# Values of two steps on end, the shifts' parts on GpSimd, and a reordered second QKV stage in a two-layer transformer kernel

## The reference, cut to what matters

```python
q = apply_rope(q, 0)
k = apply_rope(k, 0)
scores = jnp.einsum('bhqd,bhkd->bhqk', q, k) / math.sqrt(HEAD_DIM)
scores = jnp.where(causal[None, None, :, :], scores, jnp.float32(-1e+20))
attn = jax.nn.softmax(scores, axis=-1)
out = jnp.einsum('bhqk,bhkd->bhqd', attn, v)
...
scores = jnp.einsum('bhfc,bhtc->bhft', k, q)
attn = jax.nn.softmax(scores, axis=-2)
vals = jnp.einsum('bhft,bhfc->bhtc', attn, v)
```

## Time and profile before

| | us |
|---|---|
| median of three executions | 1273.25 |
| lowest, highest | 1272.96, 1280.2 |
| profiled execution | 1285.09 |
| its span (first to last instruction) | 1283.3 |

### The profile page before, as it was taken

The page is one execution under the profiler, slowest core; times in us unless marked ns, Lnnn a source line. Parts: engine busy times, 40 slices in busy tenths (PEclk is TensorE's granted clock), DMA queues, the critical chain, the costliest instruction groups (busy, mean ns, idle before and its releaser), DMA issues.

```text
span 1283.3 us, 21563 instructions
## 1 busy us (share of the span) xinstructions
PE 1192.6 (93%) x6800; PEld 744.0 (58%) x6800; DVE 915.8 (71%) x2958; ACT 661.6 (52%) x1015; POOL 396.2 (31%) x521
## 2 busy tenths in 40 slices
PE   4999999999889998999989999999998999989988
PEld 1775443444358997545878644443332889855478
DVE  5778897999527868663777798998880578676365
ACT  1732574666545644444545136666666356445542
POOL 1433431221144520115624434122123445002261
PEclk9897696999899999899999958998897999989999
DMA  9555221131001014100241742112200100430001
GB/s 301 189 147 125 84 76 26 27 78 50 2 1 52 2 34 99 60 2 1 83 166 40 194 122 76 27 27 60 68 3 1 34 19 1 99 92 2 1 10 58
DMA packets 40053, 81.44 MB, mean 63 GB/s; under 512 B 6044, under 2 KB 7580, under 8 KB 39532
## 3 DMA queue, kind: packets, MB, share of 16 engines
q1 hardware_dynamic: 39944, 80.06, 21.8%
HBM read 50.02 MB, written 28.13 MB: 61 GB/s over the span
## 4 chain that ended last, share of the span: by engine, by line
PE 71%; DVE 14%; issue 5%; DMA 4%; ACT 3%; POOL 2%; SPq 1%; DVEq 0%; ACTq 0%; POOLq 0%
PE bank L1060 17%; PE bank L927 12%; PE bank L833 6%; PE bank L835 6%; PE bank L834 6%; PE bank L1041 5%; DVE maxes L1280 5%; PE bank L819 3%; DVE unused L1276 3%; PE bank L1035 3%; PE bank L937 2%; DVE features L1209 2%; PE bank L858 2%; PE bank L909 1%; PE bank L860 1%
## 5 line engine op out<-in xcount | busy, mean ns | idle before, releaser
L1528 ACT ACTIVATE probs<-bank 128x1024 f32<-128x1024 f32 (+3 forms) x416 | 366.0, 911 | 278.3 <-PE bank L1041 195.4
L927 PE MATMUL bank<-ops 48*128 48x512 f32 (+3 forms) x960 | 315.3, 432 | 10.5 <-DVE maxes L1280 3.4
L1276 DVE CUSTOM_DVE_ANT_0 unused<-bank,causal 128x128 bf16<-128x128 f32 (+3 forms) x640 | 279.1, 486 | 44.7 <-PE bank L927 40.7
L1660 POOL TENSOR_SCALAR_AFFINE_SELECT probs<-probs 128x256 f32<-128x256 f32 (+1 forms) x256 | 119.4, 467 | 575.5 <-ACT probs L1528 574.5
L927 PEld LDWEIGHTS bank<-ops 48*128 48x128 f32 (+1 forms) x960 | 160.6, 205 | 194.3 <-DVE maxes L1276 77.3
L1060 PE MATMUL bank<-probs,v_mem 128*17 128x512 f32 (+6 forms) x1920 | 256.2, 542 | 1.4 <-ACT heads_raw L1515 0.8
L1280 DVE TENSOR_REDUCE maxes<-bank 128x1 f32<-128x512 f32 x320 | 207.2, 684 | 50.3 <-PE bank L927 49.3
L1041 PE MATMUL bank<-ops 50*128 50x512 f32 (+2 forms) x640 | 181.7, 464 | 8.0 <-DMA ops<-shiftT 4.6
L1041 PEld LDWEIGHTS bank<-ops 50*128 50x128 f32 x640 | 89.9, 205 | 68.0 <-issue 35.4
L833 PE MATMUL bank<-ops,xT 128*128 128x512 f32 (+1 forms) x288 | 114.0, 396 | 6.7 <-DVE xT L1119 2.6
L1119 DVE TENSOR_TENSOR xT<-bank,xT 128x512 fp32r<-128x512 f32 (+1 forms) x96 | 61.5, 644 | 75.5 <-ACT xT L1390 75.4
(11 more groups left out here) (128 smaller groups left out, 1903.8 us busy)
## 6 DMA issues: line engine op xcount, KB each, us to landing
query_rows_dram<-ops SPq DMA_DIRECT2D x48, 256.0 KB, 4.3
ops<-query_rows_dram SPq DMA_DIRECT2D x64, 192.0 KB, 4.4
w_odd<-staging_wqkv SPq DMA_DIRECT2D x4, 1536.0 KB, 6.8
x<-x_dram SPq DMA_DIRECT2D x16, 256.0 KB, 4.1
ops<-features SPq DMA_DIRECT2D x64, 64.0 KB, 2.0
ops<-ops SPq DMA_DIRECT2D x16, 256.0 KB, 3.0
out_dram<-x SPq DMA_DIRECT2D x16, 256.0 KB, 2.0
staging_wqkv<-wqkv_dram SPq DMA_DIRECT2D x2, 1536.0 KB, 14.2
```

Of the source, the lines that this page charges most:

```text
L927: last = mm(dst[:, h * w:(h + 1) * w], queries(a, u)[rows, t // 4, hi, t % 4 * P:(t % 4 + 1) * P], keys(a, u, hi)[rows, HALF * kp:HALF * k ...
L1276: V.tensor_tensor_reduce(unused[:, masked % 3, 0:w], part, causal[:, HALF - w:], 1.0, NEG, ALU.add, ALU.max, dst).then_inc(s["max_done"].s ...
L1528: A.activation(probs[:, e % 6, :, 0:cols], scores[:, 2 * (e % 2):2 * (e % 2) + 2, 0:cols], ACT.Exp, scale=a.scale).then_inc(s["exp"].sem, 1)
L1660: G.affine_select(out=p, in_=p, compare_op=ALU.is_ge, fill=0.0, base=0, pattern=pattern, channel_multiplier=-1).then_inc(s["masked"].sem, 1)
```

## The change

It does six things.

1. In the rotated attention the values of two steps stand on end too: at every odd step those of the steps three and two before it. The standard attention keeps its order.
2. `probs` has 8 places instead of 6.
3. The high and low part of a shift are made by POOL in the rotated attention (a copy and a subtraction, in POOL's list at the step in which the last maximum of that half is read). In both attentions the parts are those of the maximum itself, and the rows beside the keys hold minus one.
4. The two halves of a maximum are joined by a reduction over one operand (a view of both halves) in place of the maximum of two operands.
5. In the rotated attention the turning of a shift follows its last maximum by 6 banks instead of 3; `slack` goes from 4 to 1, so that as many items stand ahead of the first step as before.
6. The second QKV stage makes block (3, 0) ahead of the values, splits the first value products, and starts the ring later by another table; the second `load_shifts` of unit 0 goes ahead of the rows of block (2, 0).

```diff
-SHIFT_DELAY = 3
...
+        self.shift_delay = 6 if self.rope else 3
...
-            order = [(0, 0), (1, 0), first, (3, 0), (0, 1), (1, 1), (3, 1), second, (2, 1), (2, 0)]
-            self.ring_in = {4: (0, 0, 1, 1), 5: (1, 1, 1, 1), 7: (0, 0, 1, 1), 8: (1, 2, 2, 2), 9: (1, 2, 2, 1)}
+            order = [(0, 0), (1, 0), (3, 0), first[:2], (0, 1), (1, 1), (3, 1), first[2:], second, (2, 1), (2, 0)]
+            self.ring_in = {6: (1, 1, 1, 1), 7: (1, 1), 8: (1, 1, 1, 1), 9: (1, 2, 2, 2), 10: (1, 2, 2, 0)}
...
-A0 = Attention("rot", 32, 8, 16, 0.25, 2, True, ahead=1.07, slack=4)
+A0 = Attention("rot", 32, 8, 16, 0.25, 2, True, ahead=1.07, slack=1)
...
+PROBS = 8
...
                 load_shifts(b, QKV1, 0, 0)
-                for j, g in ((2, 1), (2, 0)):
-                    rows_of_block(b, j, g)
+                rows_of_block(b, 2, 1)
                 load_shifts(b, QKV1, 0, 1)
+                rows_of_block(b, 2, 0)
...
-                    if a.row_tiles == 2:
-                        if a.lag <= g < a.units * ns + a.lag:
-                            value(g - a.lag)
-                    elif g % 2 == 0 and g > a.lag and g - a.lag < a.units * ns:
+                    if (g - a.lag) % 2 == 1 and g > a.lag and g - a.lag < a.units * ns:
                         value(g - a.lag - 1)
                         value(g - a.lag)
...
-                    if n + 1 in a.max_banks_of:
+                    if n + 1 in a.max_banks_of and not (a.rope and n + 1 == a.max_banks_of[0]):
                         shift_parts(b, st, u, a.max_banks_of.index(n + 1))
...
                 if c == 1:
-                    V.tensor_tensor(mx, mx, maxes[:, u % 2, 1, 0:nh, 4:8], ALU.max).then_inc(s["shift_step"].sem, 1)
+                    both = maxes[:, u % 2, :, 0:nh, 4:8].rearrange("p k h t -> p h t k")
+                    mx = maxes[:, u % 2, 1, 0:nh, 0:4]
+                    V.tensor_reduce(mx.unsqueeze(3), both, AX.X, ALU.max).then_inc(s["shift_step"].sem, 1)
+                if a.rope:
+                    return
...
-                            if e >= 6:
+                            if e >= PROBS:
...
+            def shift_parts(b, u, c):
...
+                G.tensor_copy(hi, mx).then_inc(step.sem, 1)
+                pool.wait_ge(step.sem, step.at(b, 3 * u + 1 + 2 * c))
+                G.tensor_tensor(lo, mx, hi.bitcast(F32), ALU.subtract).then_inc(s["shift"].sem, 1)
...
+                    for (u, c), at in a.shift_parts_at.items():
+                        if a.rope and at == g:
+                            shift_parts(b, u, c)
```

More of the change, by code:

```diff
@@ L195, in plan_ring @@
         per = len(self.max_banks)
-        start = self.max_banks_of[0] + SHIFT_DELAY + self.slack
+        start = self.max_banks_of[0] + self.shift_delay + self.slack
         catch_up = sum(s[3] for s in self.steps[:3]) / sum(s[3] for s in self.steps)
@@ L217, in push @@
                 if n + 1 in self.max_banks_of:
-                    due_m.append([(u, self.max_banks_of.index(n + 1)), SHIFT_DELAY])
+                    due_m.append([(u, self.max_banks_of.index(n + 1)), self.shift_delay])
                 done += 1
@@ L238, in plan_ring @@
         self.ring_len = len(self.ring)
+        where = {item: s for s, step in enumerate(self.ring_at) for slot in step for item in slot}
+        self.shift_parts_at = {(u, c): where.get(("max", u, n - 1), -1)
+                               for u in range(self.units) for c, n in enumerate(self.max_banks_of)}
         self.norm_at = [i for i, item in enumerate(self.ring) if item[0] == "norm"]
-A0 = Attention("rot", 32, 8, 16, 0.25, 2, True, ahead=1.07, slack=4)
+A0 = Attention("rot", 32, 8, 16, 0.25, 2, True, ahead=1.07, slack=1)
 A1 = Attention("std", 8, 8, 32, 1.0, 1, False, ahead=1.07, slack=12)
@@ L337, in build @@
         v_mem = sb("v_mem", [P, NT * 8 * 33])
-        probs = sb("probs", [P, 6, 2, HALF])
+        probs = sb("probs", [P, PROBS, 2, HALF])
         w_odd = sb("w_odd", [P, 2, KC * 768], F32R)
@@ L772, in _ @@
                 load_ones(QKV1)
-                for j, g in ((0, 0), (1, 0), (3, 0), (0, 1), (1, 1), (3, 1)):
+                for _, j, g in [p for p in A1.products if p[0] == "qk" and p[1] != 2]:
                     rows_of_block(b, j, g)
                 load_shifts(b, QKV1, 0, 0)
-                for j, g in ((2, 1), (2, 0)):
-                    rows_of_block(b, j, g)
+                rows_of_block(b, 2, 1)
                 load_shifts(b, QKV1, 0, 1)
+                rows_of_block(b, 2, 0)
                 after(b, QKV1)
@@ L1060, in value @@
                         last = mm(heads[a.head_rows * h:a.head_rows * h + a.dim + 1, q0 - HALF * c:HALF],
-                                  v[:, j, a.kv_head(u, r, i), :], probs[:, e % 6, n, first:first + w],
+                                  v[:, j, a.kv_head(u, r, i), :], probs[:, e % PROBS, n, first:first + w],
                                   start=(j == 0), stop=(j == 4 * c + 3))
@@ L1524, in attention @@
                             act.wait_ge(s["scored"].sem, s["scored"].at(b, e + 1))
-                            if e >= 6:
-                                act.wait_ge(s["pv"].sem, s["pv"].at(b, a.step_of(e - 6) + 1))
-                            A.activation(probs[:, e % 6, :, 0:cols], scores[:, 2 * (e % 2):2 * (e % 2) + 2, 0:cols],
+                            if e >= PROBS:
+                                act.wait_ge(s["pv"].sem, s["pv"].at(b, a.step_of(e - PROBS) + 1))
+                            A.activation(probs[:, e % PROBS, :, 0:cols], scores[:, 2 * (e % 2):2 * (e % 2) + 2, 0:cols],
                                          ACT.Exp, scale=a.scale).then_inc(s["exp"].sem, 1)
@@ L1636, in chain @@
                             turn_late(b, 4)
+            def shift_parts(b, u, c):
+                a, s = A0, qs[QKV0]
+                nh, m, step = a.unit_heads, a.unit_heads * 4, s["shift_step"]
+                mx = maxes[:, u % 2, 1, 0:nh, 0:4] if c else maxes[:, u % 2, 0, 0:nh, 0:4]
+                if c == 0:
+                    pool.wait_ge(s["max_done"].sem, s["max_done"].at(b, u * a.unit_max_ops + a.max_ops_to[a.max_banks_of[c] - 1]))
+                else:
+                    pool.wait_ge(step.sem, step.at(b, 3 * u + 2))
+                if 2 * u + c >= 2:
+                    pool.wait_ge(s["shiftT"].sem, s["shiftT"].at(b, 2 * u + c - 1))
+                hi = shifts[:, c, 0:m].rearrange("p (h t) -> p h t", h=nh)
+                lo = shifts[:, c, m:2 * m].rearrange("p (h t) -> p h t", h=nh)
+                G.tensor_copy(hi, mx).then_inc(step.sem, 1)
+                pool.wait_ge(step.sem, step.at(b, 3 * u + 1 + 2 * c))
+                G.tensor_tensor(lo, mx, hi.bitcast(F32), ALU.subtract).then_inc(s["shift"].sem, 1)
             def attention(b, st):
@@ L1640, in attention @@
                 ns = len(a.steps)
-                for g in range(a.units * ns):
+                for g in range(-1, a.units * ns):
+                    for (u, c), at in a.shift_parts_at.items():
+                        if a.rope and at == g:
+                            shift_parts(b, u, c)
+                    if g < 0:
+                        continue
                     u, k_ = divmod(g, ns)
@@ L1693 @@
         "x": a["L0_attn_x"],
-        "tables": np.concatenate([np.tile(cos.T, (16, 1)), np.tile(sin.T, (16, 1))], axis=1), "ones": np.ones((2, 8 * SEQ), np.float32),
+        "tables": np.concatenate([np.tile(cos.T, (16, 1)), np.tile(sin.T, (16, 1))], axis=1), "ones": -np.ones((2, 8 * SEQ), np.float32),
         "ffn_w": a["L0_ffn_W"].T, "ffn_a": a["L0_ffn_lora_A"], "ffn_b": a["L0_ffn_lora_B"].T,
```

9 lines of the change are left out of this document (5 added, 4 removed).

## The result

The changed kernel took 1385.76 us (median of four executions, 1381.23 to 1389.45), against 1273.11 us for the kernel before: ratio 1.0881, 95% interval 1.0811 to 1.0951, 113 us more. The forecast was 1298 us, in a range from 1268 to 1324. The sign was right; the size was less than a quarter of what happened.

What follows compares the result with a forecast made beforehand. DVE and PE were taken to hold each other up through the ring of three banks. Terms 19.7 + 0.3 + 3.8 + 3.0 - 2.0 = +24.8 us on the median 1273.25 gave 1298 us, range 1268 to 1324.

Steps and rivals of the forecast that it cites:

- the clock: Rotated attention: about 12% of each 186 us stretch at half clock, unchanged there; 11.6 full-clock units x 1.7 = +19.7 us.
- The clock falls more often: Rival: PE waits more in each unit, so three more half-clock stretches on top of the sum; 1321 us, chance 0.14.
- The pairs' gaps: Rotated attention's ring: six pairs of values leave DVE idle 4.8 us a unit, for 1.96 now; unit 29.9 us.
- this case: The prediction's own case: +24.8 us on the median, 1298 us; reaching from 1283 to 1308, chance 0.60.
- PE is the limit after all: Rival: pairs shorten PE's work by at most 2.1 us a unit; 1254 us, chance 0.11.
- Gain and loss cancel: Rival: DVE's waits grow only by the 1.17 us of work it loses, unit 28.3; 1278 us, chance 0.15.
- The shifts' parts: Rotated attention: DVE loses 1.34 us a unit and gains a 0.17 us reduction, leaving 25.13 us of work.
- POOL is late nowhere but at the end of the ring: POOL's added instructions cost nothing, except at the ring's end: +0.3 us for both sequences.
- The start: Start of the rotated attention: the shift's copy moves later, so the first score is 1.9 us later; +3.8 us for two sequences.
- The end: End of the rotated attention: a cycle of two steps takes 4.7 us in place of 4.2; +3.0 us (0 to 5).
- The second QKV stage: Its end: shift rows' DMAs moved ahead, one ring bank less for the last product; -2.0 us for both sequences (0 to -7.2).

## Why the prediction was wrong

**The step that failed is the clock.** The prediction took 12% of each stretch at half clock from the kernel before, "11.6 units" at full clock, and let the change alter nothing there. The changed kernel has no unit at full clock. A middle unit grew by 7.7 us (29.5 to 37.2). Of these, 1.43 are the pairs' gaps at full clock, by the two runs with five added matmuls, less 0.17 for the shorter DVE work. The rest, some 6.4 us, comes with 18.5 us more of half clock. Single values bring all of it back; wide added matmuls bring the clock back and most of the time.

**The rival was named, and priced too low.** "The clock falls more often" had 0.14 and 1321 us, from three more stretches like the one of the earlier trace rows. What it describes is what happened, and its count was wrong: not three more in two attentions but two or three falls in every middle unit. The prediction held it against this rival that most units do without falls. But the pairs make the same stretches without values in every unit alike. What counts in these stretches was not separated: PE stands there for a part of the time (0.9 of 3.86 us), and what it makes is narrow. With pairs, five or 13 wide matmuls a unit end nearly all falls and 48 narrow ones do not, which speaks for what PE makes. In the kernel before, 16 narrow ones end them, which speaks for the standing.

The Trainium skill, TensorE: Matmul & The Clock Gate, section on psum-queue depth-cycling, puts clock changes down to short PE stops between groups of matmuls. The stretch at 239.30 agrees (0.9 us of standing). The two ahead of 919.10 show only 0.09 us of it, with modelled ends, so no run here settles the matter.

**The pairs' gaps were right.** The forecast was 1.16 us of idle DVE at each pair of 512 and 512, and 1.2 and 1.1 at the pairs of 512 and 384. At full clock, with five added matmuls, they are 1.17 and 1.04, and 1.21 and 1.13. The first narrow pair, with 0.1 forecast, has 0.60, ahead of a bank that itself waits for an added matmul. The forecast for the unit was 29.9 us (28.26 + 1.7, bounds 1.0 to 2.1); it is about 29.5 by the runs. (One sum is off: the bounds of all terms give 1280 us, and not 1283, as the lower end of this case.) Where the prediction asked for gaps of over 1 us, the changed kernel itself has them at full clock too:

```profile
236.55 0.69 DVE L1277 CUSTOM_DVE_ANT_0 unused<-bank,causal 128x512 bf16<-128x512 f32 x1 [1.04 <-PE bank L931]
...
240.07 0.42 DVE L1277 CUSTOM_DVE_ANT_0 unused<-bank,causal 128x256 bf16<-128x256 f32 x1 [1.12 <-PE bank L931]
```

**"PE is the limit after all"** is out: at full clock pairs make a unit longer, not shorter. The Trainium skill, TensorEngine Tiling (Array Packing), Key Properties, says that a change of tiling mode drains the engine, and pairs make fewer changes; if that saves time, it is less than the gaps cost. **"Gain and loss cancel"** describes single values (28.09 us with 1.03 us less DVE work), and not the pairs for which it was put forward.

**The shifts' parts.** POOL's two instructions are shorter than the bounds of 0.41 to 0.55 us, and the new reduction on DVE is near the 0.17 taken:

```profile
L1659 POOL TENSOR_TENSOR shifts<-maxes,shifts 128x16 fp32r<-128x16 f32 x32 | 7.1, 223 | 2.7
L1657 POOL CAST shifts<-maxes 128x16 fp32r<-128x16 f32 x32 | 6.3, 198 | 121.3 <-DVE maxes L1327 70.8 <-DVE maxes L1277 50.5
```

```profile
237.90 0.19 DVE L1327 TENSOR_REDUCE maxes<-maxes 128x16 f32<-128x32 f32 x1
```

That POOL is late nowhere but at the end of the ring was right as well; PE waits for it twice in the whole trace, 4.1 us together. What was missed is the other side of the late turning: with pairs, its place among the short banks carries some 28 us, by the run with the old turning.

**The start** was right: the first score waits longer than in the earlier trace rows,

```profile
116.60 0.80 PE L1045 MATMUL bank<-ops 50*128 50x512 f32 x2 [3.97 <-DMA ops<-shiftT]
```

and comes 5.5 us behind the start of the last product in place of 3.7, 1.8 us for 1.9 forecast. **The end**: eight exponentials take from 402.07 to 412.63, 10.6 us in place of 8.4, 1.1 us a pair for 0.5 forecast, part of it at half clock. **The second QKV stage** was mis-sized inside its bounds: -2.0 forecast, about -6 by the run alone (0.5% of 1276.47). The wait for the DMAs that were moved is as long as before, and what went with the gain is a shorter half-clock stretch.

## What to carry to other kernels

When a change reorders PE's list, read the list for what stands between its widest matmuls, and ask of each such stretch whether the clock has fallen behind a like one before: a price per full-clock unit is worth little if the units do not stay at full clock. To find out whether a loss is the clock or the waits, add matmuls without use at the suspected place: if the kernel gets faster, the clock had a part in the loss. If it gets slower, nothing is shown: with all banks doubled the clock still fell. And take a bundled change apart: here one part of six gained 0.5%, and another lost 7%.

## What the runs showed of the hardware that was not expected

- The granted clock fell to half behind 9.76 us in which the profile shows PE standing for 0.09 us, with modelled ends. 48 added narrow matmuls a unit left 15.7 us of half clock in a middle unit, 13 wide ones 1.0 and five wide ones 0.7. The wide ones differ in rows (128 for 48), in being made in two passes, and in where they stand; which of these counts was not separated.
- In the order with single values, 16 narrow matmuls a unit were enough to end all falls in the middle units. With pairs they were not.
- Holding the clock up cost about as much as its falls: 0.8 to 1.0 us on each middle unit of the kernel before, where the falls cost 1.2 on the mean in its trace (29.5 for 28.26).
- The first unit of each rotated attention stands at half clock for 23 to 47 us in all kernels here; added matmuls at the start did not shorten that. Why it lasts so long stays open.
